# A masked-attention decoder on one core: late loads spread over the key preparation, the bound row turned by TensorE, leftover loads inside the first sweep, the causal staircase added by VectorE

## What is computed

```
a = 0 (layer L0): x += gate * Attention(x, keys and values of the 6404 context rows)
                  then a tree-routed feed-forward that gives q, k, v of one wide attention
a = 1 (layer L1): x += gate * Attention(x, context rows and, under a causal mask, the 1024 tokens)
                  then experts, then layer L2 (linear attention from a summary K'V of the context), experts
a = 2 (layer L3): x += gate * Attention(x, context rows under the mask), then experts
```

## Time and profile before

| | |
|---|---|
| median of three runs | 3363.9 us (3363.48 to 3366.98) |
| the profiled execution: its own time, its span | 3358.68 us, 3356.9 us |
| PE busy, share of the span | 3165.0 us, 94% |
| ACT busy | 2569.8 us, 77% |
| DVE busy | 349.4 us, 10% |
| chain that ended last | PE 91%, DVE 3%, issue 1%, SPq 1%, ACTq 1%, ACT 1%, POOL 1% |

### The profile page before, as it was taken

One profiled execution on the slowest core, in us unless ns is written; L12 is line 12 of the kernel. 1 busy time (PEld: TensorE's weight loads), 2 busy tenths in 40 slices (PEclk: granted clock), 3 DMA queues, 4 the chain that ended last, 5 costly groups with the idle time before them and its releaser, 6 DMA issues.

```text
span 3356.9 us, 59763 instructions
## 1 busy us (share of the span) xinstructions
PE 3165.0 (94%) x18587; PEld 1193.6 (36%) x18587; DVE 349.4 (10%) x952; ACT 2569.8 (77%) x2979; POOL 201.5 (6%) x715
## 2 busy tenths in 40 slices
PE   6679999999989799999999998969999999999988
PEld 3322222222233522322323224645632222222256
DVE  4410000000022500000000001342210000000021
ACT  3379999999933399799798994322289999999932
POOL 2000000000000000000000000010000000000000
PEclk9889999999979989899899997989999999999979
DMA  7711111111130011011010112101001111111110
GB/s 191 200 34 37 37 37 36 37 37 37 37 91 0 14 33 37 30 37 38 29 37 31 37 37 65 33 30 35 27 28 37 37 37 37 37 37 37 35 29 28
DMA packets 147807, 145.72 MB, mean 43 GB/s; under 512 B 17800, under 2 KB 101244, under 8 KB 147724
## 3 DMA queue, kind: packets, MB, share of 16 engines
q1 hardware_dynamic: 141840, 142.57, 14.0%
q10 hardware_dynamic: 5884, 2.08, 0.3%
HBM read 115.21 MB, written 29.57 MB: 43 GB/s over the span
## 4 chain that ended last, share of the span: by engine, by line
PE 91%; DVE 3%; issue 1%; SPq 1%; ACTq 1%; ACT 1%; POOL 1%; DMA 0%; DVEq 0%; POOLq 0%
PE PS L1618 37%; PE PS L1638 32%; PE PS L626 5%; PE PS L610 5%; PE PS L612 2%; PE PS L845 2%; PE PS L833 1%; PE PS L1468 1%; PE PS L1640 1%; PE PS L1478 1%; SPq L1111 1%; PE PS L1598 1%; PE PS L1682 1%; PE PS L1683 0%; PE PS L1604 0%
## 5 line engine op out<-in xcount | busy, mean ns | idle before, releaser
L1408 ACT ACTIVATE probs<-PS 128x1024 f32<-128x1024 f32 (+1 forms) x2496 | 2279.6, 1465 | 109.4 <-PE PS L1638 59.6
L1618 PE MATMUL PS<-probs,vr 128*32 128x512 f32 (+1 forms) x9984 | 1338.3, 609 | 1.5 <-DVE accs L1842 1.5
L1638 PE MATMUL PS<-qs,kr 35*128 35x512 f32 (+1 forms) x4992 | 1160.9, 500 | 29.1 <-issue 27.6
L1638 PEld LDWEIGHTS PS<-qs,kr 35*128 35x128 f32 x4992 | 480.2, 186 | 1340.0 <-ACT probs L1408 1222.2
L1268 POOL COPY vr<-vs 128x72 f32 (+1 forms) x624 | 157.8, 253 | 2834.5 <-PE PS L1618 2474.3
L1618 PEld LDWEIGHTS PS<-probs,vr 128*32 128x32 f32 x9984 | 198.3, 108 | 319.3 <-issue 181.2
L1842 DVE COPY accs<-PS 128x512 f32<-128x512 f32 x12 | 8.3, 692 | 2385.6 <-PE PS L1604 2385.6
L653 ACT ACTIVATE probs<-PS 128x512 f32<-128x512 f32 x96 | 57.4, 598 | 130.2 <-PE PS L610 71.4
L653 ACT ACTIVATE accs<-PS 128x512 f32<-128x512 f32 x96 | 57.3, 597 | 120.6 <-PE PS L610 63.2
L610 PE MATMUL PS<-xT,wide 128*128 128x512 f32 x256 | 124.9, 607 | 0.7 <-ACT xT L339 0.7
L626 PE MATMUL PS<-wide,accs 128*128 128x128 f32 x768 | 91.6, 281 | 5.0 <-DVE kf L685 5.0
(11 more groups left out here) (272 smaller groups left out, 1214.1 us busy)
## 6 DMA issues: line engine op xcount, KB each, us to landing
kr<-key_pieces SPq DMA_DIRECT2D x1248, 64.0 KB
key_pieces<-kparts SPq DMA_DIRECT2D x36, 288.0 KB, 4.5
kr<-mask_strips SPq DMA_DIRECT2D x624, 4.0 KB
key_pieces<-probs SPq DMA_DIRECT2D x32, 288.0 KB, 4.6
vs<-values SPq DMA_DIRECT2D x2, 3672.0 KB, 15.0
values<-v_next SPq DMA_DIRECT2D x9, 432.0 KB, 5.1
wide<-in_L_ffn_w SPq DMA_DIRECT2D x28, 128.0 KB, 2.1
values<-probs SPq DMA_DIRECT2D x8, 432.0 KB, 5.4
```

Of the source, the lines that this page charges most:

```text
L1408: sc.activation(prob[n % RING][:, :, q0:], PS[:, bank:bank + 2, q0:], ACT.Exp, scale=SCALE).then_inc(p_ready, 1)
L1618: last = te.matmul(PS[32 * j:32 * j + 32, 7, q0:], vr[s.buf(c)][:, at_v:at_v + 32], prob[(n + j // 2) % RING][:, j % 2, q0:], start=fresh, ...
L1638: last = te.matmul(o, kr[b][own, p, :], qs[own, T8 // 2 * s.hh + p, 512 * s.qh + q0:512 * s.qh + 512], start=True, stop=not late)
```

## The change

1. **Loads spread.** ACT's loop over the steps is written out, and the 52 transfers of the three bursts are spread over steps 1 to 14, 2 to 7 behind each step.
2. **Bound row by PE.** The transfer of the bounds is gone. PE transposes the 16 bounds into a row behind unit u = 7, and DVE reduces it and writes the flag behind u = 9.
3. **Leftover loads in the first sweep.** The 28 transfers of the leftover keys and values go out one by one behind the key loads of blocks 3 to 30 of each attention's first sweep; SP's loop over that sweep is written out.
4. **Staircase by DVE.** The identity matmuls are gone. DVE adds `stair` to the diagonal columns of both banks of a pair in one instruction, in place in PSUM, and ACT waits for that (`s_cut`) in the late blocks.
5. **Small weights and summary moved.** The five small transposes come before the first layer norm's; DVE takes them out behind the norm; the summary's products go behind the output of a = 0 and into the feed-forward.

```diff
-            with act.Fori(0, ROUNDS) as j:
-                for off in range(1, UNROLL + 1):
-                    k_step(j, off)
-            for i in TAIL:
+            for i in range(1, NTILE):
                 k_step(None, i, last=(i == NTILE - 1))
-                if i == TAIL[0]:
-                    attention_weights()
-                if i == TAIL[1]:
-                    constant_rows()
-                if i == TAIL[2]:
-                    late_weights(act)
+                if i == 1:
+                    strips()
+                if 2 <= i < 5:
+                    attention_weights(i - 2)
+                if i == 5:
+                    summary_weights()
+                if 6 <= i < 9:
+                    net_weights(act, i - 6)
+                if i == 9:
+                    router_weights(act)
+                if i == 10:
+                    output_weights()
+                if i == 11:
+                    left_rows()
+                if 12 <= i < 15:
+                    constant_rows(i - 12)
...
-                sp.wait_ge(v_final, a + 1)
-                load_left_values()
-                sp.wait_ge(bound_ready, a + 1)
-                sp.dma_start(bound_row[0:1, :], bound[32 * a:32 * a + H, 0:1]).then_inc(bound_in, 16)
...
+                for c in range(TC, first.n):
+                    sp.wait_ge(s_ready, first.groups + 4 * (c - TC) + 4)
...
+                    load_keys(first.buf(c), c if c < FULL else c + 1, 0, kr_in[first.buf(c)])
+                    if c - TC < 8:
+                        load_left_keys((c - TC) // 4, (c - TC) // 2 % 2, (c - TC) % 2)
+                    elif c - TC < 12:
+                        load_left_strip((c - TC - 8) // 2, (c - TC) % 2)
+                    elif c - TC < 12 + H:
+                        load_left_values(c - TC - 12)
...
+                    if u == 7:
+                        pe.wait_ge(bound_ready, a + 1)
+                        te.transpose(PS[0:1, 7, 0:H], bound[32 * a:32 * a + H, 0:1], ident[...]).then_inc(bound_ps, 1)
...
+                    if u == 9:
+                        dve.wait_ge(bound_ps, a + 1)
+                        chain(v.reduce_max(bound_max[:, :], PS[0:1, 7, 0:H], X_AXIS))
+                        v.tensor_scalar(flag[0:1, a:a + 1], bound_max[:, :], (SAFE / SCALE) ** 2, None, ALU.is_ge).then_inc(flag_ready, 1)
...
-                                if late:
-                                    last = te.matmul(o[:, 0:P], ident_b[:, :], stair[:, :], start=False, stop=True)
...
+                    for c in range(FULL + 4 * s.qh, s.n):
+                        for p in range(4):
+                            n, q0 = s.groups + 4 * c + p, s.seen(c)
+                            diagonal = PS[:, 2 * (n % TC):2 * (n % TC) + 2, q0:q0 + P]
+                            dve.wait_ge(s_ready, n + 1)
+                            v.tensor_tensor(diagonal, diagonal, stair[:, :].unsqueeze(1).to_broadcast([P, 2, P]), ALU.add).then_inc(s_cut, 1)
...
+                        if s.cut(c):
+                            act.wait_ge(s_cut, s.cuts(c, p))
```

More of the change, by code:

```diff
@@ L817, in fff_pe @@
             last.then_inc(f_node, 1)
+            pe.wait_ge(gram_sb, 2)
+            te.matmul(PS[:, 6, 0:D], wv5[:, 3, :], gram_v[:, :], start=True, stop=False)
+            te.matmul(PS[:, 6, 0:D], sum_bk[:, :], wv5[:, 4, :], start=False, stop=False)
+            te.matmul(PS[:, 6, 0:D], b5[0:1, 3, :], n_bv[0:1, :], start=False, stop=True).then_inc(gram_ps, 1)
             pe.wait_ge(f_leaf, 1)
@@ L841, in out @@
                 o = PS[:, 4 + 2 * (net % 2) + half, :]
+                if net == 1 and k == 0:
+                    pe.wait_ge(gram_sb, 3)
                 if net == 2 and k == 0:
@@ L1139, in _ @@
                     home = first.buf(0)
+                    if a == 1:
+                        for b in range(2):
+                            sp.wait_ge(k_out[b], KEYS_OUT[b] + STORES)
                     sp.wait_ge(kr_in[home], KEYS_IN * (first.uses(0) + 1))
@@ L1495, in _ @@
             norms(None, NTILE - 1)
+            pe.wait_ge(w_late, WEIGHTS_LATE)
+            pe.wait_ge(v_ev, NTILE * TC)
+            pe.wait_ge(kn_ev, NTILE)
+            for i in range(2):
+                te.transpose(PS[:, 6, (2 + i) * D:(3 + i) * D], l2w[:, i, :], ident[:, :])
+            te.transpose(PS[:, 7, 3 * D:4 * D], l2w[:, 2, :], ident[:, :])
+            pe.wait_ge(rows_ready, 1)
+            te.transpose(PS[:, 4, 3 * P:3 * P + 64], mask_f[0:64, :], ident[0:64, 0:64])
+            pe.wait_ge(f_in, SMALL_IN)
+            te.transpose(PS[:, 5, 3 * P:3 * P + 96], rows_w[0:96, :], ident[0:96, 0:96]).then_inc(wprep_ps, 1)
             pe.wait_ge(wprep_ready, 2)
@@ L1637, in scores @@
                                 o = PS[:, 2 * (n % TC) + e, q0:]
-                                last = te.matmul(o, kr[b][own, p, :], qs[own, T8 // 2 * s.hh + p, 512 * s.qh + q0:512 * s.qh + 512], start=True, stop=not late)
-                                if late:
-                                    last = te.matmul(o[:, 0:P], ident_b[:, :], stair[:, :], start=False, stop=True)
+                                last = te.matmul(o, kr[b][own, p, :], qs[own, T8 // 2 * s.hh + p, 512 * s.qh + q0:512 * s.qh + 512], start=True, stop=True)
                             last.then_inc(s_ready, 1)
@@ L1684, in _ @@
                 last.then_inc(y_ps, 1)
+                if a == 0:
+                    te.matmul(PS[:, 7, 0:D], gram[:, 0:D], wv5[:, 4, :], start=True, stop=True).then_inc(gram_ps, 1)
                 between_pe(pe, a)
```

165 lines of the change are left out of this document (73 added, 92 removed).

## The result

The changed kernel takes 3258.4 us (median of four executions, 3254.3 to 3259.1), the kernel before beside it 3364.0 us (3363.5 to 3367.0): a ratio of 0.9682, 95% interval 0.9665 to 0.9698. The profiled execution took 3254.3 us, with a span of 3252.5 us; the mean granted clock of TensorE went from 0.953 to 0.968. The forecast was 3269 with a range of 3255 to 3303. 105.6 us were gained where the sum had 94.9.

A forecast was written before the change was run, and what follows sets the result against it. PE was taken as the bound, busy 94% of the span and 91% of the chain. Gains of 16.3 + 13.0 + 3.2 + 62.4 = 94.9 us took 3358.7 to 3263.8 profiled, 3269 for the median; range 3255 to 3303.

The forecast's parts named there:

- allowance of 2 us for the transfers: Key preparation: loss allowed for SP's and ACT's transfers sharing the DMA engines, 2 us, with 3.2 us at a 0.92 share.
- rule of the Trainium skill: Key preparation: SP and ACT transfers share 16 engines; bytes not hidden, so the whole 5.1 us would be lost.
- the 7.6 that I had named as a sign of being wrong: Key preparation: a pitch over 7.6 us per step would make the prediction wrong; 7.3 to 7.5 us was expected.
- Rival B: Key preparation: loads slow ACT, 8.9 us for a step with four issues, 23 us over 14 steps; 3290; chance 0.1.
- branch: Entries into the attentions: reading the flag and branching before the first scores, 4.8 us, which stays.
- Rival E: First sweeps: SP becomes the bound in 28 blocks with a leftover load, 84 in all; 3387 at 3.2 us; chance 0.03.
- first term: Late part of four sweeps of a = 1: 101.7 us shrinks to 52, 13 per sweep; gain 49.7 us.
- lower end: Late part of a sweep: if time went with the columns, groups take 1.83, 1.62, 1.17, 0.71 us; 10.7 for eight.
- second term: Behind the late parts of a = 1: the clock holds instead of falling to half; 12.7 us more gained.
- C: Late parts: DVE's add isn't hidden, 64 adds at 0.45 us on the path, 29 us; 3298; chance 0.09.
- D: Late groups are long for another reason than the identity matmuls; only the other parts count; 3331; chance 0.03.
- A: Late parts: clock falls anyway as PE waits for exponentials; 12.7 us and some 4 more gone; 3286; chance 0.2.

The follow-up runs named there:

- a_burst: Changed kernel with the small loads issued in three groups behind steps 13, 14 and 15 of the key preparation again; 3275.9 us, ratio 0.9727.
- a_pool: Changed kernel with the spread small loads issued from GpSimd's queue in place of ACT's, in the same steps; 3259.2 us, ratio 0.9689.
- a_entryold: Changed kernel with both entry edits undone: bound row by DMA, behind the 28 leftover loads on SP's queue; 3269.6 us, ratio 0.9726.
- a_leftearly: Changed kernel with the 28 leftover loads ahead of the flag again, PE's transpose of the bounds kept; 3255.1 us, ratio 0.9670.
- a_pestair: Changed kernel with the staircase added by PE's identity matmuls again, all else kept; 3327.7 us, ratio 0.9886.
- a_nomask: Changed kernel without any staircase, so DVE's add is left out and ACT waits for the scores alone; 3253.3 us, ratio 0.9679.
- b_stair: Kernel before the change with only the staircase edit: DVE adds it, PE's identity matmuls are gone; 3290.1 us, ratio 0.9771.
- a_better2: Changed kernel with constants and mask loads awaited behind steps 3 and 4, strips moved to step 9, small loads regrouped; 3255.0 us, ratio 0.9675.

## Why the prediction was right

1. **Loads spread**: forecast 16.3 (13 to 18). Right: 17 to 18 us by a_burst and by the time from step 3 on, 14.9 in the first pair of traces because step 2 ran at half clock in one and not in the other. The allowance of 2 us for the transfers holds: thirteen steps at 7.26 us and a last one like after's (139.69 to 147.74) would be 13 x 7.26 + 8.05 = 102.4 us from step 3 on, and the mean of the seven kernels with this spread is 104.5. The rule of the Trainium skill, which would have had all 5.1 us lost, is right in that the engines are shared, too dark in the size, since they weren't full to the end: 0.97 was reached in one step, where I had 0.95 as the highest. The mean pitch from step 3 to 16 is 7.46 us, as forecast, but three steps (7.65, 7.97 and 8.13) are over the 7.6 that I had named as a sign of being wrong; it holds of the mean alone. Rival B (8.9 us for each step with four issues) is out by these pitches, and a_pool has no gain from ACT without issues.
2. and 3. **Bound row and leftover loads**: forecast 13.0, 3.2 and 0; 13.6, 3.9 and 0.7 between the two traces, 11.9, 3.9 and 0.2 by a_entryold. The branch stays at 4.9 us (4.4 behind DVE). What the sum couldn't say is that the two are one gain, won by either. The leftover loads in the sweep cost nothing: the first sweep of a = 0, which holds them, takes 191.9 us in after and 192.3 in a_leftearly, which has none in it; before has 190.9 with a shorter half clock at its start (8.7 us for 11.3 and 11.0). Rival E doesn't occur.
4. **Staircase**: the mechanism was right, the size too small, 62.4 for 72.0; 2.4 more, which make the 74.4 between the traces, are a shorter half clock at the start of the attention, and luck. The first term, the late part, was put at 13 us per sweep and is 11.8: the two groups of each width take 1.83, 1.84; 1.77, 1.62; 1.30, 1.35; 1.02 and 1.07 us, so PE shrinks with the columns nearly as in my lower end, one group later. 101.7 - 47.2 = 54.5 in place of 49.7. The second term, the clock behind the late parts, was put at 12.7 and is 17.6, what is left of 72.0. I had counted exponentials behind three joints; the leftover tokens' work right at each of four joints also ran at half clock (up to the copy of the sums a sweep's end became 17.5, 16.2, 16.5 and 14.9 us shorter, 65.1 in all, 10.6 more than the late parts), and the second and third sweep got 7.0 us from the clock further in. The first term isn't free of the clock either, which the sum passes over: of before's late parts 28 us ran at half clock (from 1381.6, 1613.7, 1828.7 and 2054.0 to their ends). A group of 128 columns with its identity matmuls takes 2.24 us at full clock in a_pestair and 3.50 at half in before; I estimate from these that some 10 of the 54.5 us are the clock's. Timeline of PE in a_pestair, the scores that begin two groups following each other, with the first identity matmul, then such scores in before:

```profile
1795.48 0.32 PE L1674 MATMUL PS<-qs,kr 35*128 35x128 f32 x1
1795.74 0.23 PE L1676 MATMUL PS<-stair,ident_b 128*128 128x128 bf16 x1
...
1797.72 0.32 PE L1674 MATMUL PS<-qs,kr 35*128 35x128 f32 x1
```

```profile
1383.20 0.47 PE L1638 MATMUL PS<-qs,kr 35*128 35x128 f32 x1
...
1386.70 0.47 PE L1638 MATMUL PS<-qs,kr 35*128 35x128 f32 x1
```

DVE's add takes 0.43 us with PSUM as source and target, near the 0.41 of the row that I took it from. Rivals C and D are out, by a_nomask and b_stair; what A describes shows only when the add is doubled.
5. **Moved products**: forecast 0. The feed-forward took 181.3 us for 180.1, the way from DVE's last piece to the last query rows 17.8 for 18.1. No run moves the products back; the other parts, each read at its own place (72.0, 17.8 by a_burst, 16.0 by a_entryold), make 105.8 us of the 105.6 and leave nothing for them that could be told.

So the time came out 11 us below the forecast, at the lower end of the range, mostly by the staircase's two terms. The clock at the beginning of an attention, at half for 11 to 17 us in after and 9 to 23 in before, differs from trace to trace over the same code; it gave 2.4 us in a = 1 and took some 3 in a = 2 (17.0 us at half for 8.8).

## What to carry to other kernels

When two edits take the same small transfer from behind the same queue, they are one gain: undo each alone and both together before crediting either. Work that keeps PE busy but adds nothing (identity matmuls for a mask) can cost more than its own time, here 72 us, of which the clock has 17.6 behind the late parts and by my estimate some 10 in them; another engine with idle time takes it for nothing as long as its time per tile, 0.43 us, stays below that of the slowest engine, and at 0.80 us it began to show. Spread transfers over the steps in place of a burst on an engine that also computes, here 17 to 18 us; once they are spread, which engine issues them made no difference here.

## What the runs showed of the hardware that I had not expected

- The same instructions at the same place run at either clock in different executions: step 2 of the key preparation, 2.17 us for its key products in four traces and 4.0 to 4.2 in seven (the three kernels with another start aside), 2 us of the whole time.
- The clock fell to 0.50 in a_pestair and before while PE was shown busy for every 5 us of the stretch, and stayed at 1.00 in the same place with less, narrower work.
- An issue of a transfer isn't of fixed length: the 54 by ACT from 27 us to the end of after's key preparation took 0.26 to 1.64 us, the median 0.69, and two of constant rows in a_better2 3.39 and 1.74 us at a share of 0.91, where the same in a_burst took 0.6 to 0.7. ACT's next instruction started 0.1 us behind their end (90.86 and 90.98).
- A DMA of sixteen numbers was in use 1.7 us after its issue began (a_entryold, 172.23 to 173.91); behind 28 small loads in one queue it made the entry 12 us longer.
